# Filler matmuls left out of the pair steps that hold two or more TensorE stages

## The reference, cut to what matters

```
x = layernorm(x + splat_attention(x))            # 16 heads of 16
x = layernorm(x + cross_attention(x, ctx))       # 16 heads of 16, 120 keys
x = layernorm(x + best_of_8_experts(x))
x = layernorm(x + causal_attention(x))           # 16 heads of 16
x = layernorm(x + two_blocks(x, ctx))            # each: attention (16 heads of 32) and an MLP of 1024, gelu
x = layernorm(x + four_of_16_experts(x))
```

## Time and profile before

| | before |
|---|---|
| median of three runs | 3736.82 us |
| the profiled execution's own time | 3737.38 us |
| its span, first to last instruction | 3735.2 us |
| mean granted TensorE clock | 0.921 |
| TensorE busy (matmuls) | 3112.3 us, 83% |
| DVE busy | 2683.9 us, 72% |
| ACT busy | 2107.7 us, 56% |
| POOL busy | 975.4 us, 26% |
| streams (line 711) | 1280 matmuls, 420.7 us busy |

### The profile page before, as it was taken

The page is one execution under the profiler, slowest core; times in us unless marked ns, Lnnn a source line. Parts: engine busy times, 40 slices in busy tenths (PEclk is TensorE's granted clock), DMA queues, the critical chain, the costliest instruction groups (busy, mean ns, idle before and its releaser), DMA issues. The chain is left out here.

```text
span 3735.2 us, 89796 instructions
## 1 busy us (share of the span) xinstructions
PE 3112.3 (83%) x34864; PEld 2448.2 (66%) x34864; DVE 2683.9 (72%) x6391; ACT 2107.7 (56%) x4254; POOL 975.4 (26%) x1788
## 2 busy tenths in 40 slices
PE   1989888888888878888988888798888897989886
PEld 1767676767676757766766667676766676766664
DVE  5768686767676767777777668687776677868765
ACT  4746565555556554664565655646655556466642
POOL 0312351122232421231243222212342122124310
PEclk9989899989999989998999989999998999989987
DMA  6211212112212121121122111212121112112110
GB/s 198 70 56 57 74 56 62 41 44 63 63 57 71 50 63 43 49 68 52 47 66 64 55 54 38 71 45 72 59 69 60 38 42 70 47 61 71 60 37 6
DMA packets 362009, 221.50 MB, mean 59 GB/s; under 512 B 102497, under 2 KB 333299, under 8 KB 361587
## 3 DMA queue, kind: packets, MB, share of 16 engines
q1 hardware_dynamic: 361586, 215.76, 19.2%
HBM read 122.23 MB, written 93.32 MB: 58 GB/s over the span
## 5 line engine op out<-in xcount | busy, mean ns | idle before, releaser
L1151 ACT ACTIVATE p<-bank,p_log 128x512 f32<-128x512 f32 (+2 forms) x1280 | 749.0, 585 | 1098.8 <-PE bank L840 995.1
L1712 POOL TENSOR_TENSOR prob<-p,prob 120x256 f16<-120x256 f32 (+2 forms) x512 | 451.0, 881 | 1648.7 <-ACT prob L1152 1648.3
L1152 ACT ACTIVATE prob<-bank,p_log 128x512 f16<-128x512 f32 (+2 forms) x1280 | 750.3, 586 | 0.0
L1417 DVE TENSOR_REDUCE negm<-bank 128x2 f16<-128x512 f32 (+1 forms) x1024 | 511.2, 541 | 82.4 <-PE bank L804 78.9
L1340 DVE TENSOR_TENSOR prob<-p,prob 128x512 f16<-128x512 f32 (+2 forms) x768 | 488.1, 644 | 92.2 <-ACT prob L1152 87.8
L711 PE MATMUL bank<-w_exp,ident_h 128*128 128x512 f16 x1280 | 420.7, 413 | 95.2 <-DMA k_ring<-k_heads 79.1
L819 PE MATMUL bank<-q_ring,k_ring 80*128 80x256 f16 (+4 forms) x2048 | 443.9, 284 | 42.1 <-ACT raw L1098 15.8
L840 PE MATMUL bank<-ident_h,negm 128*128 128x256 f16 (+2 forms) x2560 | 440.3, 259 | 0.0
L1721 POOL TENSOR_SCALAR_AFFINE_SELECT probm<-prob 128x128 f16<-128x128 f16 x1024 | 329.0, 361 | 300.0 <-DVE prob L1340 300.0
L804 PEld LDWEIGHTS bank<-k_ring,q_ring 80*128 80x128 f16 (+1 forms) x2560 | 236.5, 104 | 233.3 <-issue 54.5
L804 PE MATMUL bank<-k_ring,q_ring 80*128 80x256 f16 (+4 forms) x2560 | 362.5, 259 | 32.1 <-DVE negm L1417 21.5
(11 more groups left out here) (293 smaller groups left out, 6262.4 us busy)
## 6 DMA issues: line engine op xcount, KB each, us to landing
q_ring<-q_heads SPq DMA_DIRECT2D x768, 40.0 KB, 2.2
q_heads<-q_made SPq DMA_DIRECT2D x96, 256.0 KB, 2.4
k_heads<-k_made SPq DMA_DIRECT2D x96, 256.0 KB, 2.4
q_ring<-q_heads SPq DMA_DIRECT2D x512, 48.0 KB, 2.2
k_ring<-k_heads SPq DMA_DIRECT2D x512, 40.0 KB, 2.2
q_heads<-q_made SPq DMA_DIRECT2D x144, 128.0 KB, 1.8
k_heads<-k_made SPq DMA_DIRECT2D x144, 128.0 KB, 1.8
k_ring<-k_heads SPq DMA_DIRECT2D x256, 48.0 KB, 2.2
```

The costliest lines, as they stand in the source:

```text
L1151: act(p32[0:n, g % PBUF32, 0:cols], ps[0:n, 0:cols], ACT.Exp, bias=p_log[0:n, :], scale=a.scale)
L1152: act(prob[0:n, 0, g % PBUF, 0:cols], ps[0:n, 0:cols], ACT.Exp, bias=p_log[0:n, :], scale=a.scale).then_inc(a_done, one(a_done))
L1417: v.tensor_reduce(negm[:, h * NT:(h + 1) * NT], scores[:, :].rearrange("p (t n) -> p t n", t=NT)[:, :, 0:ATTNS[k].keys], AX.X, ALU.max, ne ...
L1712: g.tensor_tensor(prob[0:n, 1, m % PBUF, 0:cols], p32[0:n, m % PBUF32, 0:cols], prob[0:n, 0, m % PBUF, 0:cols], ALU.subtract).then_inc(pp_ ...
```

## The change

The number of streams at the start of a pair step is 2 as before if the step holds no or one TensorE stage, and 0 if it holds two or more. The row scores that followed them follow the two waits directly.

```diff
+def stages_in_step(g):
+
+    return sum(len(TIMETABLE["tensor"].get(g // PAIR * TURNS + m, ())) for m in range(TURNS))
...
                         ps = slot("v", "max", g)
                         if g == pair[0]:
-                            stream(ps, STREAM_ROWS)
+                            stream(ps, STREAM_ROWS if stages_in_step(g) < 2 else 0)
```

## The result

The changed kernel takes 3758.32 us, the kernel before in the same sessions 3741.09 us (medians of nine runs each). The ratio is 1.0054, with an interval of 1.004 to 1.0067: 20 us more (15 to 25 by the interval). The forecast was 3744 us, 7 us more, with a mean granted clock of 0.901.

What follows compares the result with a forecast made beforehand. TensorE sets the end for nearly half the time, otherwise its waits for DVE norms and the key ring's DMA. 3737.38 - 39 (streams given back) + 46 (clock falls) = 3744 us, range 3698 to 3787 for 8 in 10.

Steps and rivals of the forecast that it cites:

- 22 falls' worth: One thick step in eleven newly falls to the lower clock, 6.9 us each: 152 us more there, 46 us lost.
- the four named: Thick steps at 2011.87, 2062.13, 2109.45 and 2148.78, at 1.00 though TensorE is busy at most 84 to 88%: candidates to fall.
- the named band: Thick steps at clock 1.00 with TensorE 84 to 88% busy, where new falls were expected.
- a third, 39 of 117 us: Thick steps: a third give their streams back, 79 steps of 0.49 us, 39 us gained; waits cover the rest.
- five in 15 on the chain: From 3373 us to the last step, the chain passes through the streams of five of 15 thick steps.
- the step at 2020.13: Thick step where a later wait covers the streams: TensorE stands 2.62 us until DVE's gates are there.
- 0.22 to 0.5: Loss per microsecond at the lower clock: 0.22 us with TensorE's chain share, 0.5 with all; 0.3 taken.
- the clock holds: Faster rival, 26%: thick steps stay filled enough without streams, only the 39 us gain is left, 3698 us.
- 43 falls come: Slower rival, 31%: two thick steps in 11 fall anew, 89 us lost less 39 gained, 3787 us, clock 0.88.
- the streams carry no clock and are in nobody's way: Rival, 5%: saved time goes into the next wait for key ring or norms, clock stays, 3737 us.
- the forecast's case: Gain and loss nearly cancel: 3744 us, own range 3722 to 3760, clock 0.90; chance 38%.
- the slower one: The 31% case of falls in many thick steps: slower than the kernel before by more than 0.5%, 19 us.

Runs made afterwards that it cites:

- the two runs that split the change: Kernel before with streams left out only in 90 steps of three or more stages: 0.9987; only in 148 steps with exactly two: 1.0056.
- the 116 steps: Kernel before with streams left out only in 116 thick steps that stood at the upper clock in both profiles: 3726.95 us, ratio 0.998.
- Added time: Changed kernel with 32 in place of 16 narrow matmuls (16 columns) at the start of each thick step: ratio 1.0142 to the kernel before, against 1.006.
- narrow matmuls against none: Changed kernel with 16 matmuls of 16 columns in each thick step, compared with the changed kernel itself: ratio 1.006 to the kernel before.
- all 640 steps: Kernel before with streams gone from every pair step: replaced by 16 narrow matmuls, 3813.8 us, 1.0214; with nothing in their place, 3786.22 us, 1.0139.
- the norm waits: Kernel before with 8 streams ahead of 32 transposes that wait for DVE's norm: ratio 1.0036; the same on the changed kernel: 1.0072 to the kernel before.

## Why the prediction held, and where its sum was off

**The clock: right in size, and only in part in its place.** 22 falls' worth, 152 us more at the lower clock and a mean of 0.901 were forecast; 163 us and 0.902 came (138 us and 0.903 in the profiles). The place was to be steps at 1.00 that are 84 to 88% busy. Of the four named, one fell (2110.88), and one that already fell got worse (2134.35); three stayed at 1.00. Of all 161 thick steps that stood at 1.00, 33 now have a fall: 10 of the 23 that were less than 80% busy, four of 19 at 84 to 88%, and eight of 68 at 96% or more. So a fall is likelier where TensorE did less, but the named band doesn't stand out. That most of the falls come with the steps of exactly two stages was not in the prediction; the two runs that split the change show it.

**What the streams give back: about as forecast.** The prediction took a third, 39 of 117 us, from a count of five in 15 on the chain. The steps that kept the upper clock in both profiles gave back 29% of what was held (the change), 38% (the 116 steps) and 27% (36.9 of 138.2 us in 321 steps of the kernel without any streams). Added time cost 33%. Of 117 us, 27 to 38% are 31 to 44 us, if the steps that lost the clock gave back as much as those that kept it. That so small a count came so near was partly luck, as the prediction itself said that two or eight could stand there. It also had each step give all or nothing; 22 of the 126 gave a part. The comparisons of whole runs come out lower, 21% (narrow matmuls against none) and 21 to 24% (all 640 steps), but each needs a price for the clock, which is itself worked out with a share. For the step at 2020.13 the prediction had TensorE wait for the gates of DVE; the row puts the end of that wait to ACT's `prob`. The trace has the two within 0.11 us of each other (2024.51 and 2024.62), so the sum doesn't change.

**What a microsecond at the lower clock costs: the term that was too small, as far as is known.** The prediction had 0.22 to 0.5 and took 0.3, 46 us for the falls. With 34 us given back (29%), the falls must have cost 20 + 34 = 54 us, which is 54/163 = 0.33; with 31 to 44 us given back, 51 to 64 us or 0.31 to 0.39. It isn't one price for all falls: the runs on all 640 steps give 0.23, and the falls taken away at the norm waits were worth next to nothing, since those steps wait for DVE.

So the sum was -39 + 46 = +7 where the runs have some -34 + 54 = +20 us. The mechanism came as described, gain and loss of like size, and both terms were near. Which of them carries the missing 13 us is not settled to the microsecond: by the steps it is mostly the cost of the falls, by the whole runs it would be mostly the share given back. The lengths of the steps come from one profile of each kernel. Little of what the thick steps won or lost was passed on to others: the 328 thin steps whose time at the lower clock changed by no more than 0.5 us are 3 us shorter in all.

**The rivals.** That the clock holds (3698 us) fell with the clock at 0.902. That 43 falls come (3787 us, 0.88) fell too: they would be 297 us at the lower clock, and 163 came. That the streams carry no clock and are in nobody's way fell by the runs without any, 1.0139 and 1.0214, with clocks of 0.856 and 0.872. The measured 0.54% lies just past the bound of 0.5% between the forecast's case and the slower one.

## What to carry to other kernels

Filler matmuls cost what they hold only where TensorE is late; here that was about a third of it, whether they were added or taken away. They are worth what the clock would lose without them, and that depends on where the slow stretch would fall. Left out of steps that stood at the upper clock in two profiles they gave 0.2%; left out by number of stages they cost 0.54%. Much scheduled work doesn't make a full step: those with two stages stand idle for 1.4 us of 7.6 on average. And a granted clock that rises is no gain in itself: look whether the stretch that ran slow was one that others waited for, and whether the fall is gone or has moved behind it. When a difference of some microseconds is priced by the clock, take the mean over all executions: by one profile of each, the run on 116 steps had 14 us more at the lower clock, by all of them 29, and this decides whether its result speaks against a third or for it.

## What was not expected of the hardware

The clock fell behind two waits of 0.76 and 0.88 us, with matmuls before, between and after them, where the same stretch with 0.43 us more of matmuls and a wait of 0.33 us had kept it. Sixteen matmuls of 16 columns, 0.40 us of them, kept the mean clock at 0.910 where nothing in their place gave 0.902, though two streams gave 0.923. In the step at 2110.88 they kept it at 1.00 just as the streams did. A clock of 0.935 came with a time 0.36% above that of the kernel before, and one of 0.930 with 0.43%. Fillers under a wait took a fall out of the steps that waited and brought one into the full step behind them.
